# Recommendation tower: ScalarE makes part of the one-hot units, transforms wait half by half, cycles start at odd quads, six MLP steps move ahead of the tail

## The chip, the cores and the metric

One core of a Trainium2 chip. The metric is the device time of one execution in microseconds, the median of three.

## The reference

2048 samples have 40 ids each, one into each of 40 tables of 32-wide rows. For every pair of fields the kernel computes a bilinear form with a matrix of its own, puts 16 dense values behind the 780 results, and runs a small MLP. Cut to what matters:

```python
e = jnp.stack([tbl_f[ids[:, f]] for f in range(40)], axis=1)     # (2048, 40, 32)
vi, vj = e[:, _I_IDX, :], e[:, _J_IDX, :]                        # 780 pairs
z = jnp.einsum('bke,kef,bkf->bk', vi, W, vj)                     # W: (780, 32, 32)
h = jnp.concatenate([z, dense_ctx], axis=1)                      # (2048, 796)
h = jnp.maximum(h @ W_top1 + b_top1, 0.0)                        # 512
h = jnp.maximum(h @ W_top2 + b_top2, 0.0)                        # 256
y = h @ W_top3
```

## The kernel before, in words

The samples go in four chunks of 512, which lie along the free axis. The fields go in ten groups of four, so that a group's embeddings are a tile eT of 128 x 512.

A **quad** is up to four blocks of pairs. TensorE **transforms** (L567): four fp32 matmuls on 32 rows each, two into one PSUM bank pair (half 0) and two into the next (half 1); there are three such pairs. VectorE multiplies each half by the eT of the partner group into prods (L543), two **products** of 1024 columns a quad. TensorE **reduces** (L589): four matmuls with a 0/1 matrix add the products into zps. Eight quads fill a sum, which ScalarE drains into zs (L387). A chunk has 53 quads, numbered 0 to 52; 212 in all.

Tables with 1000 rows are **hot**: a hot group isn't gathered but looked up. For each of 8 **units** VectorE compares the group's shortened ids (L409, by ScalarE) with a code and writes a one-hot tile (L493), four slots in turn; TensorE multiplies it by the table in three bf16 parts, 12 matmuls (**look-up**, L616); after unit 7 ScalarE drains the bank mlp_ps into eT (L423). The chunks have 4, 3, 2 and 2 hot groups. The other 29 (chunk, group) pairs are gathered by GpSimd, 16 indirect DMAs each, and transposed by VectorE (L500).

The **MLP** of a chunk runs while the next chunk's quads go on, in **steps** (one k of one output tile, L636), two or three in a batch, through the one bank mlp_ps, which the look-ups share. The last chunk's MLP is the **tail**, in seven banks, after the last quad.

The order is written out by hand. TensorE and ScalarE go by **cycles** of two quads, at an even number over all 212. A table SIDES gives each quad its look-ups and MLP steps, MAKES the units to be made behind its products, 2 quads ahead of the look-up for units made in chunk 0 and 4 in the others; both engines with waits work strictly in their order. Without MLP steps a cycle is transform, reduction of the quad before, look-up, transform, reduction, look-up; with steps it is transform, steps, transform, two reductions. Where a cycle starts with the first quad of a sum, its last step goes between the reductions, as zps must be drained first. A transform waits once, for the first half of the quad before it to be multiplied (`wait(pe, multiplied, 2 * at - 1)`). The hot table of group 3 lies in the room of the MLP's first weights (w1s), which ScalarE loads after the last look-up that reads it.

## Time and profile before

| | us |
|---|---|
| median of 3 runs | 696.76 (696.74 to 699.01) |
| the profiled execution | 699.06 |
| its span, first to last instruction | 697.2 |
| TensorE busy in the span | 644.0 |
| VectorE busy | 580.5 |
| ScalarE busy | 70.1 |
| GpSimd busy (gathers) | 460.5 |

Busy is the time in which an engine had an instruction in work. What follows from the rows is worked out against the span, and carried over to the median as a difference.

### The profile page before, as it was taken

The numbers are of one execution on the slowest core, as the hardware profiler recorded it, in microseconds if no ns is written. First come the engines' busy times: TensorE is split into PE (matmuls) and PEld (weight loads), VectorE is DVE, ScalarE is ACT, GpSimd is POOL, SyncE is SP. The second block draws the span as 40 slices with busy tenths as digits, with TensorE's granted clock in tenths as the row PEclk, the third lists the DMA queues.
The fourth block names the chain that finished last, engine by engine and source line by source line (L and its number), as shares of the span: only waits on it lengthen the run. The fifth ranks groups of instructions, "written<-read, shape, count | busy, mean of one in ns | idle before, by whom it ended". The sixth has DMA issues, their size and how long they took to land.

```text
span 697.2 us, 11003 instructions
## 1 busy us (share of the span) xinstructions
PE 644.0 (92%) x4800; PEld 187.3 (27%) x4800; DVE 580.5 (83%) x578; ACT 70.1 (10%) x87; POOL 460.5 (66%) x471
## 2 busy tenths in 40 slices
PE   3898988988999999999999999998999999999898
PEld 1232222222223322322222222222222222222143
DVE  6988999999978799889877889889888888888800
ACT  5502001000100100110000000100000000000002
POOL 6777777777777777777777777777777777500000
PEclk9999999999999999999999999999999999999999
DMA  8735202000000110200000200000101000000000
GB/s 322 276 98 194 69 13 74 14 13 14 13 14 15 32 58 13 74 14 13 15 13 15 76 14 14 13 14 14 16 14 15 14 14 13 12 1 1 1 0 1
DMA packets 18944, 28.28 MB, mean 41 GB/s; under 512 B 8448, under 2 KB 16016, under 8 KB 17232
## 3 DMA queue, kind: packets, MB, share of 16 engines
q0 software_dynamic: 14848, 7.63, 7.4%
q1 hardware_dynamic: 3296, 17.57, 6.5%
q10 hardware_dynamic: 752, 2.37, 0.9%
q8 instruction: 38, 0.62, 0.4%
q14 instruction: 10, 0.08, 0.0%
HBM read 27.53 MB, written 0.01 MB: 40 GB/s over the span
## 4 chain that ended last, share of the span: by engine, by line
PE 61%; DVE 34%; issue 3%; DMA 1%; ACT 1%; ACTq 0%; SPq 0%; DVEq 0%
DVE prods L543 26%; PE tps L567 25%; PE zps L589 15%; PE mlp_ps L636 15%; DVE hot L493 6%; PE tps L636 4%; PE mlp_ps L616 2%; DMA ids<-in_hot_ids 1%; DVE eT L500 1%; PE zps L576 1%; DVE parts L482 0%; DVE zs L482 0%; ACTq L467 0%; ACT ids L409 0%; DVE w1s L482 0%
## 5 line engine op out<-in xcount | busy, mean ns | idle before, releaser
L543 DVE TENSOR_TENSOR prods<-tps,eT 128x1024 f32<-128x1024 f32 (+1 forms) x440 | 495.1, 1168 | 72.5 <-PE tps L567 68.8
L371 POOL DMA_INDIRECT rows<-in_table,idx x464 | 459.9, 991 | 144.4 <-issue 141.2
L567 PE MATMUL tps<-eT,weights 32*128 32x512 f32 x1680 | 242.4, 641 | 33.4 <-DVE prods L543 31.1
L589 PE MATMUL zps<-prods,select 128*32 128x512 f32 x1680 | 217.7, 605 | 2.3 <-DVE prods L543 1.5
L567 PEld LDWEIGHTS tps<-eT,weights 32*128 32x128 f32 x1680 | 66.7, 183 | 185.3 <-DVE prods L543 146.4
L636 PE MATMUL mlp_ps<-zs,w1s 128*128 128x512 f32 x182 | 89.8, 615 | 0.0
L589 PEld LDWEIGHTS zps<-prods,select 128*32 128x32 f32 x1680 | 38.2, 108 | 159.4 <-DVE prods L543 98.7
L616 PE MATMUL mlp_ps<-hot,parts 128*32 128x512 bf16 x960 | 65.2, 389 | 14.7 <-DVE hot L493 10.9
L493 DVE TENSOR_SCALAR hot<-ids,code 128x2048 bf16<-128x2048 int16 (+1 forms) x88 | 67.4, 787 | 1.9 <-ACT ids L409 1.6
L387 ACT ACTIVATE zs<-zps 128x512 f32<-128x512 f32 x28 | 16.7, 598 | 326.3 <-PE zps L589 326.3
L636 PEld LDWEIGHTS mlp_ps<-zs,w1s 128*128 128x128 f32 x182 | 31.3, 189 | 55.1 <-issue 55.1
L616 PEld LDWEIGHTS mlp_ps<-hot,parts 128*32 128x32 bf16 x960 | 27.1, 99 | 66.4 <-issue 37.0
L636 PE MATMUL mlp_ps<-h1s,w2s 128*128 128x512 f32 x48 | 24.1, 620 | 0.0
L394 ACT ACTIVATE h1s<-mlp_ps,b1s 128x512 f32<-128x512 f32 x13 | 8.9, 688 | 145.0 <-PE mlp_ps L636 145.0
L500 DVE STREAM_TRANSPOSE eT<-rows 128x512 f32<-128x512 f32 x29 | 20.3, 701 | 0.0
L409 ACT ACTIVATE ids<-ids 128x2048 int16<-128x2048 int32 x10 | 19.0, 1903 | 2.5 <-issue 2.5
L636 PE MATMUL tps<-zs,w1s 128*128 128x512 f32 x42 | 19.2, 592 | 0.0
L423 ACT ACTIVATE eT<-mlp_ps 128x512 f32<-128x512 f32 x11 | 6.6, 597 | 70.5 <-PE mlp_ps L616 70.4
L636 PEld LDWEIGHTS mlp_ps<-h1s,w2s 128*128 128x128 f32 x48 | 8.0, 189 | 15.2 <-issue 13.7
L636 PEld LDWEIGHTS tps<-zs,w1s 128*128 128x128 f32 x42 | 8.0, 190 | 10.0 <-issue 10.0
L394 ACT ACTIVATE h2s<-mlp_ps,b2s 128x512 f32<-128x512 f32 x6 | 4.1, 688 | 60.7 <-PE mlp_ps L636 60.7
L616 PE MATMUL mlp_ps<-hot,w1s 128*32 128x512 bf16 x96 | 7.6, 440 | 0.0
(31 smaller groups left out, 50.4 us busy)
## 6 DMA issues: line engine op xcount, KB each, us to landing
ids<-in_hot_ids SPq DMA_DIRECT2D x10, 1024.0 KB
rows<-in_table,idx POOLq DMA_INDIRECT x464, 2.4
zs<-in_hot_table SPq DMA_DIRECT2D x4, 512.0 KB, 7.5
w1s<-in_w ACTq DMA_DIRECT2D x1, 1792.0 KB, 7.6
weights<-in_wt SPq DMA_DIRECT2D x1, 1088.0 KB
...
```

The lines of the kernel that those rows point to most:

```text
L371: pool.indirect_dma_start(rows[:, k % ROW_SLOTS, m * EMB:(m + 1) * EMB], None, table, bass.IndirectOffsetOnAxis(ap=idx[:, g, t, m:m + 1], ...
L387: act.activation(zs[:, t % 2, kt, :], zps[:, :], ACT.Copy).then_inc(z_drained, 1)
L394: act.activation(dst[:, m, :], banks[out_tile], ACT.Relu, bias=bias[:, m:m + 1]).then_inc(mlp_drained, 1)
L409: act.activation(ids16[:, h % 2].rearrange("p q c -> p (q c)"), wide_ids[h], ACT.Copy).then_inc(ids_short, 1)
L493: dve.tensor_scalar(hot[:, (h * UNITS + u) % HOT_SLOTS], ids16[:, h % 2] if short else ids32[:, :, :], code[:, u:u + 1], None, ALU.is_equa ...
L500: dve.transpose(eT[:, (t * GROUPS + g) % ET_SLOTS, :], rows[:, k % ROW_SLOTS, :]).then_inc(transposed, 1)
L543: last = dve.tensor_tensor(prods[:, at % PROD_SLOTS, r:to + 1, :], tps[:, pair, r % 2:to % 2 + 1, :], eT[:, (t * GROUPS + c) % ET_SLOTS, : ...
L567: last = pe.matmul(tps[:, (2 * at + half) % PAIR_BANKS, r % 2, :], weights[part, n, :], eT[part, slot, :], start=True, stop=True)
L576: pe.matmul(zps[EMB * r:EMB * (r + 1), :], place[:, r, :], dense_s[:, :], start=True, stop=False)
L589: last = pe.matmul(zps[EMB * r:EMB * (r + 1), :], select[:, off:off + EMB], prods[:, at % PROD_SLOTS, r, :], start=kt < KT - 1 and n == fi ...
L616: last = pe.matmul(mlp_ps[EMB * q:EMB * (q + 1), :], part_of[g][part][:, col:col + EMB], hot[:, at % HOT_SLOTS, q, :], start=u == 0 and pa ...
L636: last = pe.matmul(banks[out_tile], [w1s, w2s][layer][:, k, m * PART:(m + 1) * PART], [zs[:, t % 2, k, :], h1s[:, k % M1, :]][layer], star ...
```

## The change

Seven things, in the order of the diff. Chunk 1 has 4 hot groups, its group 3 first, so that w1s is free after that one; 28 pairs are gathered, and eT has 14 slots instead of 13. The cycles are, in each chunk, quad 0 alone and then the pairs (1, 2), (3, 4) and so on; the case with a step between the reductions is gone, and a cycle with a single step has its reduction ahead of it. The batches of the MLP stand in one cycle after another, in chunk 3 too, where they were spread. Six steps of the last chunk's MLP (tile 0, k from 0 to 5) stand at quads 37, 39, 41, 43, 45 and 51 of chunk 3 instead of in the tail. ScalarE makes units 0, 2, 3, 5 and 6 of chunk 1's groups and the odd ones of chunks 2 and 3, in two activations: |id - code|, and relu(1 - that), which is 1 for equal integers and 0 otherwise. All units are made 4 quads ahead. And each half of a transform waits for itself: half 0 for the products one and a half quads back, half 1 as the whole did before.

```diff
@@ -81,7 +81,7 @@
-ROW_SLOTS, ET_SLOTS, PROD_SLOTS = 6, 13, 3
+ROW_SLOTS, ET_SLOTS, PROD_SLOTS = 6, 14, 3
 PAIR_BANKS = 3
@@ -104,8 +104,9 @@
 HOT_GROUPS = len(HOT_FIELDS) // Q
-HOT_COUNT = (4, 3, 2, 2)
-HOTS = [(t, g) for t in range(CHUNKS) for g in range(HOT_COUNT[t])]
+HOT_COUNT = (4, 4, 2, 2)
+HOTS = [(t, g) for t in range(CHUNKS) for g in ((3, 0, 1, 2) if t == 1 else range(HOT_COUNT[t]))]
 GATHERED = [(t, g) for t in range(CHUNKS) for g in range(HOT_COUNT[t], GROUPS)]
@@ -126,7 +127,12 @@
     return cut
+CYCLES = [at for t in range(CHUNKS) for at in [(t * QUADS,)] + [(t * QUADS + n, t * QUADS + n + 1) for n in range(1, QUADS, 2)]]
 def plan_sides():
@@ -141,26 +147,42 @@
         hots = [h for h, (t_, _) in enumerate(HOTS) if t_ == t + 1]
-        cycles = [at for at in range(0, TOTAL, 2) if t * QUADS <= at < (t + 1) * QUADS]
+        twos = [cycle[0] for cycle in CYCLES if len(cycle) == 2 and cycle[0] // QUADS == t]
         first = 3 * M1
...
         blocks += steps[first:] + [(h, u) for h in hots[1:] for u in range(0, UNITS, 2)]
-        for k, block in enumerate(blocks):
-            at = cycles[k if hots else k * len(cycles) // len(blocks)]
+        for at, block in zip(twos, blocks):
             if isinstance(block, tuple):
...
                 sides[at] += block
+    for k, n in enumerate(EARLY_AT):
+        sides[(CHUNKS - 1) * QUADS + n].append(("mlp", CHUNKS - 1, 0, 0, k))
     return sides
+EARLY_AT = (37, 39, 41, 43, 45, 51)
 SIDES = plan_sides()
-MADE_AHEAD = (2, 4, 4, 4)
+EARLY = [("mlp", CHUNKS - 1, 0, 0, k) for k in range(len(EARLY_AT))]
+def by_scalar(h, u):
+    return HOTS[h][0] == 1 and u not in (1, 4, 7) or HOTS[h][0] > 1 and u % 2 == 1
+def made_until(h, u, scalar):
+    return sum(by_scalar(h_, u_) == scalar for h_ in range(len(HOTS)) for u_ in range(UNITS) if (h_, u_) <= (h, u))
+MADE_AHEAD = 4
 MAKES = {at: [] for at in range(TOTAL)}
@@ -168,14 +190,12 @@
         if item[0] == "hot" and item[1] >= HOT_COUNT[0]:
-            MAKES[side_at - MADE_AHEAD[side_at // QUADS]].append(item[1:])
+            MAKES[max(side_at - MADE_AHEAD, min(side_at, 4))].append(item[1:])
 def steps_of(at):
-    steps = [item for item in SIDES[at] if item[0] == "mlp"]
-    return steps, int(len(steps) > 0 and at % QUADS % PER_KT == 0)
+    return [item for item in SIDES[at] if item[0] == "mlp"]
...
@@ -405,7 +430,8 @@
                 act.wait_ge(hot_ids_loaded[h % 2], 16 * (h // 2 + 1))
-                wait(act, hot_made, (h - 1) * UNITS)
+                if h >= 2:
+                    act.wait_ge(hot_made_dve, made_until(h - 2, UNITS - 1, False))
                 act.activation(ids16[:, h % 2].rearrange("p q c -> p (q c)"), wide_ids[h],
@@ -415,6 +441,17 @@
                 act.activation(part_of[g][part], raw_parts[g], ACT.Copy).then_inc(rounded, 1)
+            def make_unit(h, u):
+                if u == [by_scalar(h, u_) for u_ in range(UNITS)].index(True):
+                    act.wait_ge(ids_short, h + 1)
+                act.wait_ge(hot_used, h * UNITS + u - HOT_SLOTS + 1)
+                columns = hot[:, (h * UNITS + u) % HOT_SLOTS].rearrange("p q c -> p (q c)")
+                act.activation(columns, ids16[:, h % 2].rearrange("p q c -> p (q c)"), ACT.Abs,
+                               bias=minus_code[:, u:u + 1]).then_inc(distances, 1)
+                act.wait_ge(distances, made_until(h, u, True))
+                act.activation(columns, columns, ACT.Relu, scale=-1.0, bias=ones[:, 0:1]).then_inc(hot_made_act, 1)
             def drain_hot(h):
@@ -445,26 +482,31 @@
             round_part(3, 1)
+            act.wait_ge(code_built, 1)
+            act.activation(minus_code[:, :], code[:, :], ACT.Copy, scale=-1.0).then_inc(codes_turned, 1)
+            act.wait_ge(codes_turned, 1)
+            act.wait_ge(consts_built, 2 + Q)
             shorten(3)
-            for at in range(0, TOTAL, 2):
+            for cycle in CYCLES:
+                at = cycle[0]
                 if at in SHORTENED_AT:
                     shorten(SHORTENED_AT[at])
-                if at == QUADS // 2 * 2:
+                if at == QUADS:
                     act.wait_ge(mlp_loaded, 16 * 5)
-                steps, between = steps_of(at)
-                if not between:
-                    drain_tiles(steps)
+                drain_tiles(steps_of(at))
                 drain_sums(at - 1)
-                if between:
-                    drain_tiles(steps)
-                drain_sums(at)
-                for kind, *step in SIDES[at] + SIDES[at + 1]:
+                if len(cycle) == 2:
+                    drain_sums(at)
+                for kind, *step in [item for quad in cycle for item in SIDES[quad]]:
                     if kind == "hot" and step[1] == UNITS - 1:
                         drain_hot(step[0])
-                        if step[0] == HOT_COUNT[0] - 1:
+                        if HOTS[step[0]] == (1, HOT_GROUPS - 1):
                             for dst, src in ((w1s, w1), (w2s, w2), (w3s, w3), (b1s, b1), (b2s, b2)):
                                 act.dma_start(dst[:], src).then_inc(mlp_loaded, 16)
+                for unit in [unit for quad in cycle for unit in MAKES[quad]]:
+                    if by_scalar(*unit):
+                        make_unit(*unit)
             drain_z(CHUNKS - 1, KT - 1)
@@ -487,11 +529,11 @@
                     dve.wait_ge(code_built, 1)
-                elif u == (2 if h == 0 else 0):
+                elif u == (2 if h == 0 else [by_scalar(h, u_) for u_ in range(UNITS)].index(False)):
                     dve.wait_ge(ids_short, h + 1)
...
                 dve.tensor_scalar(hot[:, (h * UNITS + u) % HOT_SLOTS], ids16[:, h % 2] if short else ids32[:, :, :],
-                                  code[:, u:u + 1], None, ALU.is_equal).then_inc(hot_made, 1)
+                                  code[:, u:u + 1], None, ALU.is_equal).then_inc(hot_made_dve, 1)
             def transpose(k):
...
@@ -558,8 +602,9 @@
                 groups_there(pe, t, n)
-                wait(pe, multiplied, 2 * at - 1)
                 for half in range(2):
+                    wait(pe, multiplied, 2 * at + half - PAIR_BANKS + 1)
                     for r in (2 * half, 2 * half + 1):
@@ -604,9 +649,13 @@
                     bank_free(("hot", h))
-                pe.wait_ge(hot_made, at + 1)
+                if by_scalar(h, u):
+                    pe.wait_ge(hot_made_act, made_until(h, u, True))
+                else:
+                    pe.wait_ge(hot_made_dve, made_until(h, u, False))
                 for part in range(PARTS_OF):
@@ -647,30 +696,33 @@
             pe.wait_ge(consts_built, 1 + Q)
-            for at in range(0, TOTAL, 2):
-                steps, between = steps_of(at)
-                if at == QUADS // 2 * 2:
+            for cycle in CYCLES:
+                at = cycle[0]
+                steps = steps_of(at)
+                if at == QUADS:
                     pe.wait_ge(mlp_loaded, 16 * 5)
+                together = len(steps) > 1
                 transform(at)
-                for _, t, layer, m, k in steps[:len(steps) - between]:
+                if not together and at > 0:
+                    reduce(at - 1)
+                for _, t, layer, m, k in steps:
                     mlp(t, between_banks, layer, m, k)
-                if not steps and at > 0:
+                look_ups(at)
+                if len(cycle) == 2:
+                    transform(at + 1)
+                if together:
                     reduce(at - 1)
-                look_ups(at)
-                transform(at + 1)
-                if steps:
-                    reduce(at - 1)
-                for _, t, layer, m, k in steps[len(steps) - between:]:
-                    mlp(t, between_banks, layer, m, k)
-                reduce(at)
-                look_ups(at + 1)
+                if len(cycle) == 2:
+                    reduce(at)
+                    look_ups(at + 1)
             reduce(TOTAL - 1)
...
                     for m in range(outs):
-                        mlp(CHUNKS - 1, last_banks, layer, m, k)
+                        if ("mlp", CHUNKS - 1, layer, m, k) not in EARLY:
+                            mlp(CHUNKS - 1, last_banks, layer, m, k)
```

ScalarE at the start of chunk 0, before. The ids (L409) are those of hot group 3 of chunk 0 and, five DMA issues later, of the first hot group of chunk 1:

```order
L409 ACTIVATE ids<-ids 128x2048 [waits hot_made,hot_ids_loaded1]
L423 ACTIVATE eT<-mlp_ps 128x512 [waits hot_used] x2
L467 DMA w1s<-in_w 128x3584
L467 DMA w2s<-in_w 128x1024
L467 DMA w3s<-in_w 128x2
L467 DMA b1s<-in_b 128x4
L467 DMA b2s<-in_b 128x2
L409 ACTIVATE ids<-ids 128x2048 [waits hot_made,hot_ids_loaded0]
L387 ACTIVATE zs<-zps 128x512 [waits reduced,remainder]
```

The same place in the changed kernel, up to the first drained sum (L412); L451 and L454 are the two activations of a unit:

```order
L435 ACTIVATE ids<-ids 128x2048 [waits hot_ids_loaded1,hot_made_dve,consts_built,codes_turned]
L460 ACTIVATE eT<-mlp_ps 128x512 [waits hot_used]
L435 ACTIVATE ids<-ids 128x2048 [waits hot_made_dve,hot_ids_loaded0]
L460 ACTIVATE eT<-mlp_ps 128x512 [waits hot_used]
L451 ACTIVATE hot<-ids,minus_code 128x2048 [waits hot_used,ids_short]
L454 ACTIVATE hot<-hot,ones 128x2048 [waits distances]
L451 ACTIVATE hot<-ids,minus_code 128x2048 [waits hot_used]
L454 ACTIVATE hot<-hot,ones 128x2048 [waits distances]
L451 ACTIVATE hot<-ids,minus_code 128x2048 [waits hot_used]
L454 ACTIVATE hot<-hot,ones 128x2048 [waits distances]
L412 ACTIVATE zs<-zps 128x512 [waits reduced,remainder]
```

The second conversion stands ahead of the second drain now, the DMA issues are further down (behind the drain of the first hot group of chunk 1), and three units stand ahead of the first sum.

TensorE at the start of chunk 2, before. L567 is the transform, L636 an MLP step, L589 the reduction:

```order
L567 MATMUL tps<-eT,weights 128x512 x4
L636 MATMUL mlp_ps<-zs,w1s 128x512
L567 MATMUL tps<-eT,weights 128x512 x4
L589 MATMUL zps<-prods,select 32x512 x4
L636 MATMUL mlp_ps<-zs,w1s 128x512
L589 MATMUL zps<-prods,select 32x512 x4
L567 MATMUL tps<-eT,weights 128x512 x2
L636 MATMUL mlp_ps<-zs,w1s 128x512 x2
L567 MATMUL tps<-eT,weights 128x512 x4
L589 MATMUL zps<-prods,select 32x512 x6
L567 MATMUL tps<-eT,weights 128x512 x4
```

And in the changed kernel, from chunk 2's second quad on:

```order
L612 MATMUL tps<-eT,weights 128x512 x4
L685 MATMUL mlp_ps<-zs,w1s 128x512 x2
L612 MATMUL tps<-eT,weights 128x512 x2
L634 MATMUL zps<-prods,select 32x512 x8
L612 MATMUL tps<-eT,weights 128x512 x4
L685 MATMUL mlp_ps<-zs,w1s 128x512 x2
L612 MATMUL tps<-eT,weights 128x512 x4
```

The step between two reductions is gone; each cycle is transform, steps, transform, reductions of two quads.

TensorE around quad 43 of chunk 3, before:

```order
L567 MATMUL tps<-eT,weights 128x512 x4
L589 MATMUL zps<-prods,select 32x512 x4
L567 MATMUL tps<-eT,weights 128x512 x4
L589 MATMUL zps<-prods,select 32x512 x4
L567 MATMUL tps<-eT,weights 128x512 x4
L636 MATMUL mlp_ps<-h1s,w2s 128x512 x2
L567 MATMUL tps<-eT,weights 128x512 x4
L589 MATMUL zps<-prods,select 32x512 x8
```

And in the changed kernel, around the first two of the six steps that came out of the tail, quads 36 to 39:

```order
L612 MATMUL tps<-eT,weights 128x512 x4
L634 MATMUL zps<-prods,select 32x512 x4
L685 MATMUL mlp_ps<-zs,w1s 128x512
L612 MATMUL tps<-eT,weights 128x512 x4
L634 MATMUL zps<-prods,select 32x512 x4
L612 MATMUL tps<-eT,weights 128x512 x4
L634 MATMUL zps<-prods,select 32x512 x4
L685 MATMUL mlp_ps<-zs,w1s 128x512
L612 MATMUL tps<-eT,weights 128x512 x4
```

A batch of two steps of the MLP of chunk 2 stood here in every second or third cycle; now a single step of the last chunk's does.

TensorE with its waits, a quad of chunk 0 with a look-up, before:

```order
L567 MATMUL tps<-eT,weights 128x512 [waits multiplied]
L567 MATMUL tps<-eT,weights 128x512 x3
L589 MATMUL zps<-prods,select 32x512 [waits multiplied]
L589 MATMUL zps<-prods,select 32x512 x3
L616 MATMUL mlp_ps<-hot,parts 32x512 [waits hot_made,hot_drained]
L616 MATMUL mlp_ps<-hot,parts 32x512 x11
```

And in the changed kernel:

```order
L612 MATMUL tps<-eT,weights 128x512 [waits multiplied]
L612 MATMUL tps<-eT,weights 128x512
L612 MATMUL tps<-eT,weights 128x512 [waits multiplied]
L612 MATMUL tps<-eT,weights 128x512
L634 MATMUL zps<-prods,select 32x512 [waits multiplied]
L634 MATMUL zps<-prods,select 32x512 x3
```

The transform's four matmuls have a second wait in their midst, on the same semaphore.

## Rows read from the trace of the kernel before

**Rows 1.** The page, busy time of each engine, share of the span and instructions.
```profile
PE 644.0 (92%) x4800; PEld 187.3 (27%) x4800; DVE 580.5 (83%) x578; ACT 70.1 (10%) x87; POOL 460.5 (66%) x471
```

**Rows 2.** Windows: chunk 0 from quad 5, chunk 3, the tail (clock, DMA, GB/s last).
```profile
55.20:189.20 134.00, 119.84 (x1060) 31.90 (x1064) 130.25 (x131) 8.98 (x11) 102.89 (x103) 0.99 0.17 43
...
510.20:661.50 151.30, 143.44 (x928) 39.03 (x920) 128.55 (x118) 8.59 (x14) 72.34 (x77) 1.00 0.06 9
661.50:697.20 35.70, 32.89 (x96) 13.96 (x96) 0.00 (x0) 5.00 (x8) 0.00 (x0) 1.00 0.00 1
```

**Rows 3.** Groups by line and form, ScalarE (busy us, mean ns | idle before).
```profile
L409 ACT ACTIVATE ids<-ids 128x2048 int16<-128x2048 int32 x10 | 19.0, 1903 | 2.5 <-issue 2.5
L387 ACT ACTIVATE zs<-zps 128x512 f32<-128x512 f32 x28 | 16.7, 598 | 326.3 <-PE zps L589 326.3
L394 ACT ACTIVATE h1s<-mlp_ps,b1s 128x512 f32<-128x512 f32 x13 | 8.9, 688 | 145.0 <-PE mlp_ps L636 145.0
...
L417 ACT ACT_TABLE_LOAD x1 | 1.3, 1283 | 0.8 <-PEq L731 0.8
```

**Rows 4.** Timeline of TensorE, chunk 0, quads 42 and 43 (start, us).
```profile
163.46 1.14 PE L567 MATMUL tps<-eT,weights 32*128 32x512 f32 x8 [0.47 <-DVE prods L543]
164.59 1.06 PE L589 MATMUL zps<-prods,select 128*32 128x512 f32 x8
165.47 0.83 PE L616 MATMUL mlp_ps<-hot,parts 128*32 128x512 bf16 x12
166.23 1.14 PE L567 MATMUL tps<-eT,weights 32*128 32x512 f32 x8
```

**Rows 5.** Timeline of VectorE, the same stretch.
```profile
162.19 4.80 DVE L543 TENSOR_TENSOR prods<-tps,eT 128x1024 f32<-128x1024 f32 x4
166.91 0.74 DVE L493 TENSOR_SCALAR hot<-ids,code 128x2048 bf16<-128x2048 int16 x1
167.57 4.80 DVE L543 TENSOR_TENSOR prods<-tps,eT 128x1024 f32<-128x1024 f32 x4
```

**Rows 6.** Timeline of TensorE, chunk 1, a cycle with two MLP steps.
```profile
295.04 1.98 PE L636 MATMUL mlp_ps<-h1s,w2s 128*128 128x512 f32 x4
296.95 1.14 PE L567 MATMUL tps<-eT,weights 32*128 32x512 f32 x8
298.02 1.92 PE L589 MATMUL zps<-prods,select 128*32 128x512 f32 x16
299.88 1.14 PE L567 MATMUL tps<-eT,weights 32*128 32x512 f32 x8
```

**Rows 7.** Timeline of VectorE, chunk 1, quads with look-up and unit.
```profile
319.50 2.34 DVE L543 TENSOR_TENSOR prods<-tps,eT 128x1024 f32<-128x1024 f32 x2
...
325.35 2.35 DVE L543 TENSOR_TENSOR prods<-tps,eT 128x1024 f32<-128x1024 f32 x2
```

**Rows 8.** Timelines of ScalarE and VectorE at 52 us; window of 38 to 40.
```profile
52.46 1.91 ACT L409 ACTIVATE ids<-ids 128x2048 int16<-128x2048 int32 x1 [2.47 <-issue]
...
54.41 0.87 DVE L493 TENSOR_SCALAR hot<-ids,code 128x2048 bf16<-128x2048 int16 x1 [1.61 <-ACT ids L409]
...
38.00:40.00 2.00, 1.78 (x12) 0.46 (x12) 2.00 (x4) 0.00 (x0) 1.54 (x2) 0.94 0.15 27
```

**Rows 9.** Timelines, chunk 2: VectorE around 375 us, TensorE at 351.
```profile
373.20 4.81 DVE L543 TENSOR_TENSOR prods<-tps,eT 128x1024 f32<-128x1024 f32 x4 [0.64 <-PE tps L567]
379.77 2.36 DVE L543 TENSOR_TENSOR prods<-tps,eT 128x1024 f32<-128x1024 f32 x2 [1.76 <-PE tps L567]
...
351.34 1.13 PE L636 MATMUL mlp_ps<-zs,w1s 128*128 128x512 f32 x2
352.39 1.07 PE L589 MATMUL zps<-prods,select 128*32 128x512 f32 x8
```

**Rows 10.** Timeline of TensorE, the tail.
```profile
679.81 1.02 PE L636 MATMUL mlp_ps<-zs,w1s 128*128 128x512 f32 x2
...
683.24 1.02 PE L636 MATMUL mlp_ps<-zs,w1s 128*128 128x512 f32 x2
```

19 lines of the change are left out of this document (13 added, 6 removed).

## The prediction

> **What bounds the kernel now.** I read the page's busy line first [rows 1]: TensorE has a matmul in flight for 92% of the span, VectorE works for 83%, ScalarE for 10%. So neither of the first two can be made faster alone for long, and ScalarE is free. An average hides who waits where, so next come the stretches [rows 2]: chunk 0 from its quad 5 on takes 134.0 us, in which VectorE works 130.3; chunk 3 takes 151.3 with TensorE at 143.4; after the last product TensorE works alone for 35.7 us. To price one step I read the timeline and take the time from the start of one block to the start of the next, with nothing between: reduction to look-up 0.88, look-up to transform 0.76 [rows 4]; transform to the next block 1.07 (296.95 to 298.02), two MLP steps 1.91, two reductions 1.86 [rows 6]; one MLP step alone 1.05 and a further one 0.86 [rows 9, 10].
>
> Two loops come out of it. Where VectorE has its 0.66 us unit in a quad, the quad takes 2.93, the next one 2.45, since the group of four products begins at 162.19, the unit at 166.91, the next group at 167.57 [rows 5]. But 166.91 - 162.19 is 4.72 for two quads, so the second needs only 4.72 - 2.45 = 2.27 of VectorE. The other 0.18 is a stall, and [rows 4] show it: TensorE waits 0.47 for a product, so it was free at 162.99, and starts the transform at 163.46, and the next product can't start before 164.6. In cycles with two MLP steps TensorE never stops: 1.07 + 1.91 + 1.07 + 1.86 = 5.91 for two quads [rows 6], against 2 x 2.27 = 4.54 on VectorE.
>
> **The change, part by part.** (a) *First units of chunk 1.* VectorE waits 1.61 us at 54.41 for the shortened ids, and ScalarE started those at 52.46 only because it had stood 2.47 us behind five DMA issues [rows 8]. The ids themselves had come by about 38: from there the DMA engines are at 0.15 [rows 8]. The change shortens them ahead of the drain of group 3 and moves the five issues to the end of group (1, 3), some 12 quads on. That takes out 1.6 at least, one unit (0.66) goes to ScalarE, and the transform behind it isn't late. I take 3.0, with 1.6 and 4 as bounds.
>
> (b) *Chunk 0.* Units per look-up rise: 32 look-ups instead of 24 in 46 quads, 12 of their units on VectorE. A plain quad can now take VectorE's own 2.27, as the first half of a transform waits for products one and a half quads back. A quad with a look-up is set by the round product, reduction, look-up, transform, product: 0.14 + 0.88 + 0.76 + 1.07 + 0.07 = 2.92 after a plain one (0.14 and 0.07 are my estimates of the gaps before and after TensorE's part, from 163.46, where it starts some 0.05 after the product that began at 162.19 and takes 1.22, and from its end at 164.60), and TensorE's 1.07 + 0.88 + 0.76 = 2.72 after another look-up. VectorE's unit vanishes in the gap that this leaves. The pattern is two look-ups and a plain quad: 14 x 2.27 + 14 x 2.92 + 18 x 2.72 = 121.6. Before: 24 x 2.93 + 22 x 2.45 = 124.2. So 2.6 less, of which 2.0 to 2.5 go again: the dense rows' four matmuls (about one reduction, 0.9) lose their cover, and at quad 40 the drain of group (1, 1) stands behind the drain of quads 32 to 39 on ScalarE while the next look-up wants that bank: two drains of 0.60 [rows 3] and their gaps, 1.5. Net -0.5. Eight more look-ups therefore cost nothing to speak of; had they come on top it would be 8 x 0.76 = 6.1, the upper bound here.
>
> (c) *ScalarE's price.* No row shows Abs or a scaled Relu on 2048 columns. The nearest is the ids' Copy of 2048 columns, 1.90; a bias operand adds 0.688 - 0.598 = 0.09 [rows 3]. So 2 x 1.99 and two semaphore gaps, 4.1 a unit; the bounds are 3.9 and, if the second pass drags, 4.7. Chunk 0 holds 20 such units, 82 us, beside three conversions (5.7), four group drains (2.4), seven sum drains (4.2) and the five DMA issues (3): 97 of about 122 us. It fits, and a unit is made four quads, some 10.6 us, ahead.
>
> ScalarE shows one table load, of 1.28 us [rows 3], and the order of the changed program has no second one. The Trainium skill (ScalarE: Activation LUTs, What ACT_TABLE_LOAD costs) charges some 2.66 us for every switch to another table set, which would be over 5 us more a unit, 20 of them in chunk 0; but the same page (Table sets: the hidden batching unit) has relu, copy and abs in every set. By the first alone the sum would turn into a loss; by the second and the order nothing changes.
>
> (d) *Chunks 1 and 2, units.* Half of 16 units each leave VectorE. In the four quads with both a unit and a look-up, VectorE's two quads take 5.85 (319.50 to 325.35) [rows 7] and TensorE's 2 x 2.72 = 5.44: 0.41 a pair, two pairs a group, four groups, 3.3. In the pairs ahead (unit with MLP steps) both are near 5.9, and a transpose there (0.63) is in the way once or so a group; with one unit less TensorE's 5.91 covers it: 4 x 0.65 = 2.6. Together with small change -6.4; -3.3 if only the first half holds.
>
> (e) *Cycles that start at odd quads.* In chunk 2 a cycle with MLP steps that starts at the first quad of a sum splits its steps around the reductions: 373.20 to 379.77 is 6.57 [rows 9] against 5.91. The diff starts all cycles at n odd, so that this pattern is gone: three cycles at 0.66 and one with three steps at about 0.3, -2.3. Six plain quads at the chunks' ends fall from 2.45 to 2.27: -1.0.
>
> (f) *Chunk 3.* Its 17 batches now stand in 17 cycles in a row, then six cycles with one early step, three with none. By the rows: first quad 2.3; 12 x 5.91 + 4 x 6.77 (three steps) + 5.3 (the last batch, of short matmuls) = 103.3; a cycle with one step 2.27 + (0.14 + 1.0 + 1.05 + 1.07 + 0.07 = 3.33) = 5.60, six of them 33.6; three plain ones with the dense rows 3 x 4.54 + 1.0 = 14.6. Sum 153.8, against 151.3 [rows 2]: +2.5. So an early step costs about what it saves, and what pays for part of it is the split wait.
>
> (g) *Tail.* Each of the seven groups of four steps takes 683.24 - 679.81 = 3.43, 0.86 a step [rows 10]; six go: -5.1.
>
> (h) *Rest.* 28 gathered groups instead of 29, and a 14th slot: gathers wait for no slot before (GpSimd's idle time is its own issue gaps) and end long ahead of chunk 3's end, as GpSimd works 72.3 us in its 151.3 [rows 2]. Nothing. The cost of the added wait inside a transform: a second reduction follows a first in 0.86 to 1.0 with its own wait between [rows 6], so a wait that is met costs nothing; I take 0, the upper bound being 0.05 on each of 212 transforms, of which about 7 would show.
>
> Sum: -3.0 - 0.5 - 6.4 - 2.3 - 1.0 + 2.5 - 5.1 = -15.8. The profiled execution took 699.06 with a span of 697.2, the median is 696.76; the difference is carried over whole: 696.76 - 15.8 = 681.0, and I say 681.5.
>
> **Rivals.** *A, the halves don't come apart for free* (chance 0.10): the four matmuls of a transform run side by side, 8 records in 1.14 us [rows 4]. If the wait in their midst lets the second pair start late even when it is met, TensorE-bound cycles grow. For it: no row has a wait inside a transform. Against: the reductions of [rows 6]. At 0.05 each, +7 and the loss of (b) and (e)'s plain quads, +2: 691.
>
> *B, VectorE's relief is worth nothing* (0.08), as TensorE is busy anyway: only (a), (e)'s cycles, (f) and (g) remain, -3.0 - 2.3 + 2.5 - 5.1 and half of (f)'s plain quads: about -7, 690. For it the 92% of [rows 1]; against it the 5.85 against 5.44.
>
> *C, ScalarE is late* (0.05), which ends on the other side: chunk 0 leaves (122 - 15.3) / 20 = 5.3 us a unit. Up to there a late unit costs a few us; beyond it each us more a unit costs 20. At 6.1 us a unit the gain is gone, at 6.5 the time is 681.5 + 24 = 706. It needs activations at over 3 us where the nearest takes 1.90. The switch of tables of (c) is in this chance.
>
> *D, the change does all this and the clock falls* (0.02): [rows 8] show the granted clock at 0.94 from 38 to 40 after TensorE had idled at the start; more such stretches late would add some us; nothing points to them.
>
> **How the numbers follow.** My forecast has 0.75, with a range of its own of 677 to 686: (a) from -1.6 to -4, (b) up to 2 off each way, (d) down to -3.3, a unit at 4.7 us +2. Rivals A and B reach to 691 and are taken in, so that 676 to 690 leaves out C, part of A, and a little below. About 0.5%, 3.5 us, is what a measurement of this kernel tells from no change. Below 693.3 lie the forecast, B, most of A: 0.89; within 0.5% 0.06 (A with a larger price, C near its limit), slower 0.05 (C).
>
> **What would show it.** ScalarE's two new groups at about 2.0 us each, 36 of either, and ScalarE busy about 215 us. VectorE's product groups of four without a unit 4.6 long, not 4.8, in plain stretches. The wait of 1.61 at 54 us gone, and quad 6 about 3 us earlier. In chunk 0 VectorE waits for transforms in look-up quads, 0.4 to 0.7 each. In chunk 2 no cycle of 6.6. Last product to last instruction 30.6 instead of 35.7, and chunk 3 longer by 2 to 3. It would be wrong if TensorE's transform groups in MLP cycles grow beyond 1.07, or if look-ups wait for ScalarE in more places than one.

## The result and the profile after

The changed kernel takes 680.3 us (680.12 to 680.44, four runs), the kernel before beside it 697.8 (four runs, two at 696.7 and two at 698.9 and 699.0): ratio 0.974, 95% interval 0.9725 to 0.9759. The profiled execution took 680.44 with a span of 678.6, that of before 699.06 with 697.2.

The page of the changed kernel: the span, the busy line, and the groups that answer to [rows 1] and [rows 3]. In it L586 is the products, L612 the transforms, L634 the reductions, L665 the look-ups, L451 and L454 the two passes of a ScalarE unit, L412 the drain of a sum and L460 that of a looked-up group. In the variants below these numbers shift by a few lines, and the tile names stay.

```profile
span 678.6 us, 11237 instructions
PE 657.7 (97%) x4896; PEld 200.5 (30%) x4896; DVE 559.3 (82%) x550; ACT 213.9 (32%) x162; POOL 438.8 (65%) x455
L586 DVE TENSOR_TENSOR prods<-tps,eT 128x1024 f32<-128x1024 f32 (+1 forms) x440 | 492.9, 1169 | 81.5 <-PE tps L612 80.7
L451 ACT ACTIVATE hot<-ids,minus_code 128x2048 bf16<-128x2048 int16 x36 | 71.8, 1994 | 13.9 <-PE mlp_ps L665 12.2
L454 ACT ACTIVATE hot<-hot,ones 128x2048 bf16<-128x2048 bf16 x36 | 72.1, 2003 | 1.2
```

TensorE went from 92% to 97%. Read this with one caution: the wait now stands in the midst of a transform, and a transform that waits there is shown as one long group and counts as busy.

To see where the 18.6 us of span came from I cut both traces at the start of VectorE's first product of quad 0, quad 8, and of each chunk, and asked for windows. Before, quads 0 to 7, 8 to 52, chunks 1 and 2 (window, its length, then busy time of PE, PEld, DVE, ACT, POOL, the granted clock, DMA share, GB/s); chunk 3 and the tail are [rows 2]:

```profile
30.90:64.98 34.08, 29.89 (x312) 9.50 (x304) 29.41 (x34) 5.97 (x5) 26.46 (x26) 0.90 0.52 182
64.98:189.17 124.19, 111.29 (x996) 29.64 (x992) 121.26 (x121) 8.98 (x11) 95.22 (x96) 1.00 0.14 31
189.17:347.99 158.82, 154.90 (x1129) 45.16 (x1122) 138.00 (x133) 13.38 (x18) 121.31 (x124) 1.00 0.13 27
347.99:510.24 162.25, 156.23 (x1132) 44.38 (x1135) 139.25 (x135) 13.27 (x18) 123.52 (x128) 1.00 0.11 21
```

The same windows of the changed kernel, with chunk 3 and the tail:

```profile
31.45:60.39 28.94, 28.71 (x312) 9.69 (x304) 28.30 (x33) 17.62 (x12) 22.54 (x22) 1.00 0.42 145
60.39:183.13 122.74, 121.34 (x1088) 36.54 (x1080) 113.72 (x110) 77.83 (x48) 93.17 (x98) 1.00 0.21 59
183.13:338.29 155.16, 155.15 (x1130) 46.12 (x1128) 132.06 (x125) 44.96 (x34) 117.96 (x123) 1.00 0.13 28
338.29:493.45 155.16, 155.15 (x1130) 46.13 (x1128) 133.24 (x128) 44.96 (x34) 117.96 (x123) 1.00 0.11 21
493.45:648.02 154.57, 152.92 (x942) 43.84 (x940) 127.72 (x118) 8.58 (x14) 64.94 (x69) 1.00 0.06 8
648.02:678.60 30.58, 27.74 (x84) 11.69 (x84) 0.00 (x1) 5.00 (x8) 0.00 (x0) 0.98 0.00 0
```

The second number of each row is the length of the stretch. From before to changed it moves by -5.1 in quads 0 to 7 (which start 0.55 later), -1.4 in the rest of chunk 0, -3.7 in chunk 1, -7.1 in chunk 2, +3.3 in chunk 3 and -5.1 in the tail. The first row of before also has a granted clock of 0.90, where the changed kernel has 1.00.

### The profile page after: what moved, and what is told of

Read it like the earlier page. It is cut to its first block, busy times and chain, and to the rows that moved or that the text cites. A ratio compares the mean times of both kernels' runs of the same rounds, so it can differ in the third digit from the quotient of the medians.

```text
span 678.6 us, 11237 instructions
## 1 busy us (share of the span) xinstructions
PE 657.7 (97%) x4896; PEld 200.5 (30%) x4896; DVE 559.3 (82%) x550; ACT 213.9 (32%) x162; POOL 438.8 (65%) x455
## 4 chain that ended last, share of the span: by engine, by line
PE 94%; DVE 3%; DMA 1%; issue 1%; ACT 0%; SPq 0%; DVEq 0%
PE tps L612 35%; PE zps L634 30%; PE mlp_ps L685 16%; PE mlp_ps L665 8%; PE tps L685 4%; DVE hot L535 1%; DMA ids<-in_hot_ids 1%; DVE prods L586 1%; PE zps L621 1%; DVE zs L524 0%; PE mlp_ps L690 0%; DVE parts L524 0%; DVE w1s L524 0%; ACT eT L460 0%; ACT h2s L419 0%
## 5 line engine op out<-in xcount | busy, mean ns | idle before, releaser
L586 DVE TENSOR_TENSOR prods<-tps,eT 128x1024 f32<-128x1024 f32 (+1 forms) x440 | 492.9, 1169 | 81.5 <-PE tps L612 80.7
L396 POOL DMA_INDIRECT rows<-in_table,idx x448 | 438.1, 978 | 139.5 <-issue 136.3
L612 PE MATMUL tps<-eT,weights 32*128 32x512 f32 x1680 | 258.4, 640 | 1.0 <-ACT eT L460 0.8
L634 PE MATMUL zps<-prods,select 128*32 128x512 f32 x1680 | 215.2, 602 | 1.9 <-DVE prods L586 1.5
L612 PEld LDWEIGHTS tps<-eT,weights 32*128 32x128 f32 x1680 | 77.0, 182 | 149.9 <-DVE prods L586 84.1
L634 PEld LDWEIGHTS zps<-prods,select 128*32 128x32 f32 x1680 | 38.6, 108 | 157.8 <-DVE prods L586 91.7
L665 PE MATMUL mlp_ps<-hot,parts 128*32 128x512 bf16 x960 | 66.3, 395 | 15.2 <-DVE hot L535 11.1
L412 ACT ACTIVATE zs<-zps 128x512 f32<-128x512 f32 x28 | 16.7, 597 | 193.6 <-PE zps L634 193.6
L451 ACT ACTIVATE hot<-ids,minus_code 128x2048 bf16<-128x2048 int16 x36 | 71.8, 1994 | 13.9 <-PE mlp_ps L665 12.2
L454 ACT ACTIVATE hot<-hot,ones 128x2048 bf16<-128x2048 bf16 x36 | 72.1, 2003 | 1.2
L665 PEld LDWEIGHTS mlp_ps<-hot,parts 128*32 128x32 bf16 x960 | 27.6, 100 | 66.9 <-issue 33.9
L535 DVE TENSOR_SCALAR hot<-ids,code 128x2048 bf16<-128x2048 int16 (+1 forms) x60 | 44.6, 772 | 1.1 <-DMA ids<-in_hot_ids 0.9
L435 ACT ACTIVATE ids<-ids 128x2048 int16<-128x2048 int32 x11 | 20.9, 1902 | 2.4 <-DMA ids<-in_hot_ids 2.3
L460 ACT ACTIVATE eT<-mlp_ps 128x512 f32<-128x512 f32 x12 | 7.2, 597 | 38.3 <-PE mlp_ps L665 38.2
L665 PE MATMUL mlp_ps<-hot,w1s 128*32 128x512 bf16 x192 | 13.0, 379 | 0.0
```

Source lines behind the costliest of these rows:

```text
L396: pool.indirect_dma_start(rows[:, k % ROW_SLOTS, m * EMB:(m + 1) * EMB], None, table, bass.IndirectOffsetOnAxis(ap=idx[:, g, t, m:m + 1], ...
L412: act.activation(zs[:, t % 2, kt, :], zps[:, :], ACT.Copy).then_inc(z_drained, 1)
L435: act.activation(ids16[:, h % 2].rearrange("p q c -> p (q c)"), wide_ids[h], ACT.Copy).then_inc(ids_short, 1)
L451: act.activation(columns, ids16[:, h % 2].rearrange("p q c -> p (q c)"), ACT.Abs, bias=minus_code[:, u:u + 1]).then_inc(distances, 1)
L454: act.activation(columns, columns, ACT.Relu, scale=-1.0, bias=ones[:, 0:1]).then_inc(hot_made_act, 1)
L535: dve.tensor_scalar(hot[:, (h * UNITS + u) % HOT_SLOTS], ids16[:, h % 2] if short else ids32[:, :, :], code[:, u:u + 1], None, ALU.is_equa ...
```

## Experiments

**Five kernels on chips with pauses.** These were to be compared by their times.

e1, the split wait undone in the changed kernel:
```diff
-                    wait(pe, multiplied, 2 * at + half - PAIR_BANKS + 1)
+                    if half == 0:
+                        wait(pe, multiplied, 2 * at - 1)
```


> The changed kernel, but a transform again waits once, ahead of its first half, for the products of two quads back (the split wait alone is undone). My theory is that of a loop in which the 0.18 us lost in a plain quad is partly given back in the look-up quads behind it: about +2.3 us against the changed kernel, mostly in chunk 0 and in the single-step cycles of chunk 3. Rival, as the prediction had summed it: each plain quad counts for itself, 0.18 x 14 in chunk 0, 0.18 x 12 at the chunks' ends and 0.14 in each of six cycles with one early step, about +5.5. Rival A of the prediction (a wait in the midst of a transform costs 0.05 us even when it is met): -7 to -10 us, since 212 waits go, less what the stall costs again.

e2, the split wait alone, in the kernel before:
```diff
-                wait(pe, multiplied, 2 * at - 1)
                 for half in range(2):
+                    wait(pe, multiplied, 2 * at + half - 2)
```


> The kernel before with one part of the change: a transform waits for the products of each of its halves apart. Loop theory: about -5 us against before (the second quad of each pair in chunks 0 to 3 no longer stalls, of which a part is only moved into the next quad). Rival, each quad for itself: 22 x 0.18 in chunk 0 and some 25 plain or look-up quads in chunks 1 to 3, about -9. Rival B (VectorE's or TensorE's relief is worth nothing): 0 to -1. Rival A (the split costs something itself): positive, up to +7.

e3, `EARLY_AT = ()` in the changed kernel:


> The changed kernel with all 28 MLP steps of the last batch behind the last product, no early steps in chunk 3. The prediction said that an early step costs about what it saves. By its rows: tail +5.1, and in chunk 3 six single-step cycles of 5.60 become plain pairs of 4.54, -6.4: -1.3 us against the changed kernel. Rival, the early steps are hidden work and pay: +5.1 for the tail with chunk 3 unchanged, between +3 and +5.

e4, `together = len(steps) > 0` in the changed kernel:


> The changed kernel, with cycles of one early step ordered as those of two (transform, step, transform, then both reductions, where now the first reduction comes ahead of the step). Loop theory: VectorE's next product then waits for transform, step, transform alone and not for the reduction too; six cycles shrink from 5.6 to 5.1: about -3 us against the changed kernel. Rival, what an early step costs is TensorE time and not its place: 0, or +1 if the two reductions behind one another hold up the product buffers.

e6, `by_scalar` always False in the changed kernel:


> The changed kernel with all units made on VectorE (32 + 32 units, ScalarE makes none); orders, early ids, split wait, odd cycles, early steps as changed. Theory of the prediction: VectorE's second unit in a look-up pair shows. Chunk 0 has then 20 units more on VectorE (13.2 us of work, of which about 6 fall into gaps that TensorE leaves anyway), chunks 1 and 2 lose the 6.4 us of term (d) and a little of the plain quads: +11 to +12 us against the changed kernel, 692. Rival B of the prediction (VectorE's relief is worth nothing, as TensorE is busy anyway): 0 to +2.

Measured: on these chips the kernel before takes 1124 to 1126 us, and the ratios to it are e1 1.004 (1.0007 to 1.0077), e2 1.007 (1.0033 to 1.0104), e3 1.004 (1.0000 to 1.0072), e4 1.010 (1.0033 to 1.0161), e6 0.995 (0.9909 to 0.9991). No expectation can be read from that. The timeline of e1 shows why:

```profile
301.32 0.83 PE L666 MATMUL mlp_ps<-hot,parts 128*32 128x512 bf16 x12
302.08 1.14 PE L613 MATMUL tps<-eT,weights 32*128 32x512 f32 x8
...
308.55 2.00 ACT L451 ACTIVATE hot<-ids,minus_code 128x2048 bf16<-128x2048 int16 x1 [4.19 <-remote]
...
312.71 1.22 DVE L586 TENSOR_TENSOR prods<-tps,eT 128x1024 f32<-128x1024 f32 x1 [9.76 <-remote]
...
314.08 2.09 PE L613 MATMUL tps<-eT,weights 32*128 32x512 f32 x8 [9.86 <-issue]
```

TensorE, VectorE and ScalarE stand for 4 to 10 us, while GpSimd goes on with a gather every 1.25 us. The order of the waits shows where a pause starts. ScalarE's next unit needs the slot that the look-up of 301.32 frees, and VectorE's product needs the transform of 302.08. By the trace both were through by 303.2, but their semaphores are updated only at 308.46 and 312.68, and each engine starts at once then. TensorE's own next transform waits for that product and starts when it ends. So it is TensorE's signal that comes late; what holds it back is not shown. Over the whole span the clock is down to 0.82. Such pauses come at about the same quads in each of these runs (14, 21, 28, 35, 42 of chunk 0), and none of over 6 us begins after the last gather, which ends at 947 to 963 us. So the last 36 quads are undisturbed, and where the code is the same they repeat the first chip's to 0.01 us (103.17 us in e6 and in the changed kernel). Windows from quad 37 of chunk 3 to the last product, in the changed kernel, e1, e3 and e4, and the tail of e3:

```profile
603.86:648.02 44.16, 42.52 (x270) 11.18 (x268) 37.75 (x36) 1.20 (x2) 0.00 (x0) 1.00 0.00 1
```
```profile
1049.62:1093.98 44.36, 40.34 (x268) 9.16 (x268) 38.42 (x35) 1.19 (x2) 0.00 (x0) 1.00 0.00 1
```
```profile
1047.60:1086.02 38.42, 36.96 (x258) 9.76 (x256) 37.48 (x36) 1.19 (x2) 0.00 (x0) 1.00 0.00 1
1086.02:1121.80 35.78, 32.89 (x96) 13.97 (x96) 0.00 (x0) 5.00 (x8) 0.00 (x0) 1.00 0.00 0
```
```profile
1045.41:1087.08 41.67, 41.25 (x270) 11.98 (x268) 37.63 (x36) 1.19 (x2) 0.00 (x0) 1.00 0.00 1
```

e3: without early steps these quads are 5.74 shorter and the tail 5.2 longer, so the six early steps cost 0.6 more than they save (1.3 was expected). The rival (hidden work that pays) falls. e4: -2.5, where -3 was expected; so part of what an early step costs is its place in the order. A single-step cycle takes 3.36 + 2.27 = 5.63 in the changed kernel, 2.27 + 3.10 = 5.37 in e4. e1: +0.2 over 16 quads, and the single-step cycle is 3.18 + 2.45, again 5.63: what the second quad gains by the split wait, the first one gives back. For e2 the last 36 quads point the same way in the kernel before: 100.08 against 101.62, -1.5, where the shortened quads gain 1.95 and those behind them give back 0.5. The whole of e1's +2.3 and of e2's -5 was not read here; z2 below measures the former. e6 is disturbed too, but quads 40 and 42 of chunk 2 stand clear in it: with the unit back on VectorE they take 2.89 and 2.93, in the changed kernel 2.42 and 2.43, and quad 41 keeps its 2.92 or 2.93. That is some 0.5 for a pair with a unit and a look-up, where term (d) had 0.41.

**Are the gathers the cause of the pauses?** Two kernels with the same cut, after and before:
```diff
-            for k, (t, g) in enumerate(GATHERED):
+            for k, (t, g) in enumerate(GATHERED[:ROW_SLOTS]):
...
-                dve.wait_ge(rows_gathered[k % ROW_SLOTS], (k // ROW_SLOTS + 1) * (16 * GATHERS))
+                dve.wait_ge(rows_gathered[k % ROW_SLOTS], 16 * GATHERS)
```


> The changed kernel, but only the first six of its 28 groups are gathered (96 of 448 indirect DMAs); the 22 later transposes read whatever the six row slots hold, so from chunk 0 on part of the numbers are stale. On the chips of the runs so far the kernel before takes 1124 us instead of 697, and their traces show pauses in which TensorE, VectorE and ScalarE all stand, none of them after the last gather. Theory: the pauses come with the indirect DMAs, so with six groups they end at about 150 us: 680 to 710 us plus what the first 130 us lose, some 700 to 780. Rival: the pauses belong to the chip and not to the gathers (code that comes late), then about 1100 again. No theory of the change itself is tested by this kernel alone; with its partner it gives the difference of the two kernels without the pauses.

> The kernel before, with the same cut: only the first six of 29 groups gathered, the later ones stale. If gathers carry the pauses: its difference to the changed kernel with the same cut should be the 17.5 us measured on the first chip, less what the disturbed first 130 us hide: 10 to 20 us. Rival: the change gains only in the one state, and the difference is within 3 us here.

Measured: 785.2 us (781.8 to 790.1; 700 to 780 was expected) and 797.4 (796.4 to 798.6), a difference of 12.2, on a chip where the kernel before takes 1126.6. The clock shows where the pauses end, in n1:

```profile
PEclk9875555799999999999999999999999999999999
```

Quads 1 and 2 alone take 47.5 and 50.1 us there, and from the ninth slice on (156 us) nothing is disturbed. So on these chips the pauses come with the indirect DMAs. In the last of them TensorE doesn't quite stand still: from 99 to 136 us it lets through one matmul of a look-up every 2.80 us, and the last gather ends at 132.24:

```profile
127.17 0.59 PE L665 MATMUL mlp_ps<-hot,w1s 128*32 128x512 bf16 x1 [2.21 <-issue]
129.97 0.59 PE L665 MATMUL mlp_ps<-hot,w1s 128*32 128x512 bf16 x1 [2.21 <-issue]
```

And the change keeps its gain: chunks 1 and 2 of n1, then of n2:

```profile
284.70:439.70 155.00, 154.99 (x1129) 46.06 (x1128) 131.92 (x125) 44.97 (x34) 0.00 (x0) 1.00 0.04 15
439.70:594.70 155.00, 154.99 (x1130) 46.06 (x1128) 133.10 (x126) 44.97 (x34) 0.00 (x0) 1.00 0.03 8
```
```profile
287.80:446.10 158.30, 154.88 (x1129) 45.20 (x1122) 137.30 (x134) 13.37 (x18) 0.00 (x0) 1.00 0.04 15
446.10:607.60 161.50, 156.15 (x1132) 44.25 (x1135) 138.07 (x135) 13.26 (x18) 0.00 (x0) 1.00 0.02 8
```

**Four kernels without any gather.** Each has, besides its edit:
```diff
-                for m in range(GATHERS):
-                    pool.indirect_dma_start(
...
+                pool.memset(rows[:, k % ROW_SLOTS, :], 0.5).then_inc(rows_gathered[k % ROW_SLOTS], 16)
```

z1, three edits that the readings so far point to:
```diff
-EARLY_AT = (37, 39, 41, 43, 45, 51)
+EARLY_AT = (37, 37, 39, 39, 51, 51)
...
-                together = len(steps) > 1
+                together = len(steps) > 0
...
-                drain_sums(at - 1)
-                if len(cycle) == 2:
-                    drain_sums(at)
-                for kind, *step in [item for quad in cycle for item in SIDES[quad]]:
-                    if kind == "hot" and step[1] == UNITS - 1:
-                        drain_hot(step[0])
+                for quad in cycle:
+                    if quad > at:
+                        drain_sums(at)
+                    elif at > 0:
+                        drain_sums(at - 1)
+                    for kind, *step in SIDES[quad]:
+                        if kind == "hot" and step[1] == UNITS - 1:
+                            drain_hot(step[0])
```


> The changed kernel without any gather (six row slots are filled once with a constant and every transpose reads one of them: all gathered embeddings are left out), and with three edits. The six early steps stand in three cycles of two (quads 37, 39, 51 of chunk 3) instead of six of one; a cycle with any step does both reductions behind the second transform; ScalarE drains a looked-up group that ends in a cycle's first quad ahead of the sum that the same cycle ends. If the pauses come with the indirect DMAs alone, this run has none, and quads 9 to 38 of chunk 0 and all of chunks 1 and 2 last as in the changed kernel on the first chip (155.2 us each). Expected of the edits: quad 40 of chunk 0 falls from 4.17 to about 2.7 (-1.5); in chunk 3 three cycles of 5.91 and three of 4.58 stand for six of 5.63, -2.3; 680.3 - 3.8 = 676.5 us if nothing else differs. Rival: the stall at quad 40 is not ScalarE's order but TensorE's own, then 0 there and about 678.

Measured: 675.65 us (675.14 to 676.36), where 676.5 was expected. There are no pauses, and chunks 1 and 2 take 155.04 each, as on the first chip; so these kernels can be read against the first chip's traces quad by quad. Quad 40 takes 2.78 instead of 4.17. The timelines at that place, first the changed kernel:

```profile
147.61 0.60 ACT L412 ACTIVATE zs<-zps 128x512 f32<-128x512 f32 x1 [9.40 <-PE zps L634]
148.11 0.59 ACT L460 ACTIVATE eT<-mlp_ps 128x512 f32<-128x512 f32 x1
...
148.75 0.83 PE L665 MATMUL mlp_ps<-hot,parts 128*32 128x512 bf16 x12 [1.21 <-ACT eT L460]
```
and z1:
```profile
145.97 0.60 ACT L456 ACTIVATE eT<-mlp_ps 128x512 f32<-128x512 f32 x1 [7.29 <-PE mlp_ps L662]
...
147.81 0.83 PE L662 MATMUL mlp_ps<-hot,parts 128*32 128x512 bf16 x12
```

The group's drain no longer stands behind the sum's, and the look-up starts at once. Chunk 3 takes 151.78, 2.8 less.

z2, one wait, as e1:


> The changed kernel without any gather (rows filled with a constant, gathered embeddings left out), and a transform waits once again, ahead of its first half. Read quad by quad against the changed kernel. Loop theory: a plain quad takes 2.45 instead of 2.27, but the next look-up quad gives most of that back (TensorE's round is shorter by what it waited), so chunk 0 is longer by 0.9, chunks 1 and 2 by 0.4 each, chunk 3 by 0.5, together +2.3: 682 to 683 us. Rival, the prediction's sum, where each plain quad counts by itself: chunk 0 +2.5, all +5.5. Rival A (a wait met in the midst of a transform costs something): quads with MLP steps get shorter than 2.93 and 2.98.

Measured: 682.47 us (682.39 to 682.52), +2.2 with a first product 0.5 earlier. Its chunk 0, then chunk 1, against 151.68 (28.94 + 122.74) and 155.16:

```profile
30.93:183.56 152.63, 142.33 (x1400) 40.93 (x1392) 142.71 (x143) 95.44 (x59) 0.00 (x0) 1.00 0.17 62
...
183.56:339.23 155.67, 153.62 (x1132) 45.09 (x1128) 132.14 (x124) 44.95 (x34) 0.00 (x0) 1.00 0.04 15
```

By chunk it is +0.9, +0.5, +0.5 and +0.6, as the loop theory has it, and not 5.5. Against the chunks of n1, which is without gathers there as z2 is, it is +1.0, +0.6, +0.6 and +0.6, so the split wait is worth 2.5 to 2.8 us. A plain quad takes 2.45 for 2.27, and the look-up quad behind it 2.78 for 2.95. Quads with MLP steps keep their length, so a met wait in the midst of a transform costs nothing: rival A falls. TensorE's busy time is 142.3 in chunk 0, against 150.1 (28.71 + 121.34) in the changed kernel: that is the caution above in numbers.

z3, an edit for each of three chunks:
```diff
-CYCLES = [at for t in range(CHUNKS) for at in [(t * QUADS,)] + [(t * QUADS + n, t * QUADS + n + 1) for n in range(1, QUADS, 2)]]
+CYCLES = [at for t in range(CHUNKS) for at in [(t * QUADS,)] * (t != 2) + [(t * QUADS + n, t * QUADS + n + 1) for n in range(int(t != 2), QUADS - 1, 2)] + [(t * QUADS + QUADS - 1,)] * (t == 2)]
...
-    return HOTS[h][0] == 1 and u not in (1, 4, 7) or HOTS[h][0] > 1 and u % 2 == 1
+    return HOTS[h][0] == 2 or HOTS[h][0] == 3 and u % 2 == 1
```


> The changed kernel without any gather (gathered embeddings left out), and a different edit in each of three chunks, read by the lengths of the chunks (in the changed kernel 151.7, 155.1, 155.1). Chunk 0: VectorE makes all 32 units of chunk 1: theory of relief +6 (the second unit of a pair shows), rival B 0 to +1. Chunk 1: ScalarE makes all 16 units of chunk 2 instead of 8: a group of eight then takes 8 x 4.05 = 32 us where eight quads take 22, so look-ups wait for ScalarE, +8 a group, +16 in all; rival: the four quads of lead and ScalarE's idle time take it up, 0 to +4. Chunk 2: cycles start at even quads again, the last quad alone: +2.3 by the prediction's term (e), up to +5 as the split cycles also shift the look-up pairs; rival 0.

Measured, 708.6 us, chunks 0, 1 and 2:
```profile
30.70:187.89 157.19, 154.35 (x1396) 47.64 (x1384) 153.79 (x162) 17.55 (x19) 0.00 (x0) 1.00 0.16 59
187.89:359.95 172.06, 158.67 (x1131) 45.39 (x1129) 127.29 (x117) 75.46 (x50) 0.00 (x0) 0.98 0.04 13
359.95:520.04 160.09, 156.43 (x1130) 45.74 (x1128) 133.16 (x127) 44.93 (x34) 0.00 (x0) 1.00 0.02 8
```

Chunk 0 is 5.5 longer (+6 was expected): with all units VectorE works 153.8 of 157.2, so its relief was worth 5.5 us for 20 units, and rival B falls. Chunk 2 is 4.9 longer, twice term (e)'s 2.3. It doesn't isolate that term, as even cycles here lack the step between the reductions that the kernel before had, and as the look-up pairs shift too. Chunk 1 is 16.9 longer, close to the 16 that were expected, but by luck: ScalarE is busy for less than half of it. The two groups of look-ups, which run at ScalarE's 3.93 a unit, bring +3.4 and +4.6 and not 8 each, and 8.9 come from one quad (49, 12.6 instead of 3.7), which the timeline of ScalarE, TensorE and VectorE shows:

```profile
341.81 1.99 ACT L447 ACTIVATE hot<-ids,minus_code 128x2048 bf16<-128x2048 int16 x1
343.83 2.00 ACT L450 ACTIVATE hot<-hot,ones 128x2048 bf16<-128x2048 bf16 x1
345.74 0.58 ACT L408 ACTIVATE zs<-zps 128x512 f32<-128x512 f32 x1
...
346.37 1.93 PE L617 MATMUL zps<-dense_s,place 16*32 16x512 f32 x8 [6.44 <-ACT zs L408]
...
352.57 2.42 DVE L582 TENSOR_TENSOR prods<-tps,eT 128x1024 f32<-128x1024 f32 x3 [10.25 <-PE tps L608]
```

The sum drain of quads 40 to 47 stands behind the late units in ScalarE's queue, and TensorE's next reduction needs it. After the 6.44 us in which TensorE stood, the granted clock of the two windows from 342 to 354 is 0.72 and 0.71, and the blocks from the dense rows to the next transform take 5.0 us (346.37 to 351.37) that take 2.2 in the changed kernel. So some 2.8 of the 8.9 are the clock.

z4, the early ids alone, in the kernel before (`max(at // 2 * 2 - 4, 2)` for 4 in `SHORTENED_AT`):


> The kernel before without any gather (gathered embeddings left out), and ScalarE shortens the ids of chunk 1's first group at quad 2 instead of quad 4, ahead of the drain of group 3 and of its five DMA issues. Read quads 3 to 8 against the kernel before (starts 45.9, 50.4, 55.2, 58.3, 62.0, 65.0). Theory: only the 1.61 us wait at 54.4 goes, quad 4 from 4.76 to 3.1, and the stretch at half clock that follows TensorE's idling there (quad 6, 3.72) goes with it, -2.4 in all. Rival: the gain of the changed kernel at this place is the clock alone (quad 3, 4.57 against 2.99), and the early ids bring nothing where quad 3 still takes 4.57. About 694 us, with nothing else changed.

Measured: 694.1 us (692.4 to 694.3). Quad 4 takes 2.93 instead of 4.76 (-1.8) and quad 6 2.89 instead of 3.72 (-0.8), -2.6 in all, where the theory had -2.4. Quad 3 takes 3.04 instead of 4.57 (-1.5), so that the rival could not be read here; z1 settles it, where quad 3 takes 4.57 and quads 4 and 6 still take 2.93 and 2.96. The windows of 36 to 44 us tell quad 3 apart. Before:
```profile
36.00:40.00 4.00, 2.73 (x32) 0.74 (x24) 4.00 (x5) 0.60 (x1) 3.09 (x4) 0.97 0.50 185
40.00:44.00 4.00, 4.00 (x48) 1.76 (x44) 4.00 (x7) 0.00 (x0) 3.09 (x4) 0.60 0.08 12
```
z4:
```profile
36.00:40.00 4.00, 2.73 (x32) 0.74 (x24) 4.00 (x5) 1.67 (x2) 0.00 (x0) 1.00 0.41 168
40.00:44.00 4.00, 4.00 (x66) 1.67 (x60) 4.00 (x7) 0.84 (x1) 0.00 (x0) 1.00 0.54 190
```
z1, with the changed kernel's start:
```profile
40.00:44.00 4.00, 4.00 (x53) 1.65 (x42) 4.00 (x7) 0.00 (x0) 0.00 (x0) 0.65 0.72 256
```

TensorE had worked 2.73 of the 4 us ahead in before and in z4 alike, and the clock fell in one and not in the other; it fell in z1 (4.57 for quad 3), and not in the changed kernel (2.99). So the fall at quad 3 is not the change's, and it is worth some 1.6 us either way. Four runs of before at two levels, 696.7 and 699.0, with the profiled one at the upper, fit that. Such a fall isn't bound to that place: the profiled z4 has one at quad 41 of chunk 2, after TensorE had stood for 1.67 us, and its chunk 2 takes 163.15 where n2's takes 161.50. The window:
```profile
467.60:471.10 3.50, 3.50 (x16) 0.75 (x20) 3.04 (x4) 0.00 (x0) 0.00 (x0) 0.51 0.00 0
```

e9, the three edits of z1 in the whole kernel with all gathers:


> The whole changed kernel, with all gathers, and the three edits of the run without gathers (early steps in pairs, both reductions behind the second transform, a looked-up group drained ahead of the sum). On these chips the pauses hide a difference of 4 us, so the ratio to before should lie near 1.00 as that of the other variants; behind the last gather it should be exact: from quad 36 of chunk 3 to the end 71.9 us instead of 74.8 in the changed kernel. Rival: with the gathers the pairs lose what they gained, 74 to 75.

Measured: 1122.9 us (1117.1 to 1132.5) against 1125.5 (1106.7 to 1137.5), which the scatter doesn't tell apart, on a chip with pauses; behind the last gather it is as expected, 41.36 instead of 44.16 to the last product:

```profile
1047.58:1088.94 41.36, 40.74 (x270) 11.30 (x268) 37.82 (x36) 1.19 (x2) 0.00 (x0) 1.00 0.00 1
```

## Why the prediction was right

681.5 was said and 680.3 measured; against the lower level of before the change is -16.4, where the sum said -15.8. Term by term:

- (a) -3.0 for the start. The windows show -5.1 + 0.55 = -4.6, of which 1.6 is the clock at quad 3. z4 shows the early ids alone at -1.8 (quad 4) and -0.8 (quad 6, where the clock no longer falls); the last 0.4 was not tried apart. The mechanism held, and the size is the 3.0 that was said once the fall of the clock at quad 3 is taken off. That 0.8 of it is a gain in clock the prediction had not named.
- (b) -0.5, measured -1.4. The stall at quad 40 was forecast at 1.5, and z1 removes 1.4 of it. Without gathers the stretch takes 123.66 before (z4, n2) and 122.59 in the changed kernel (n1), -1.1; the other 0.4 goes with the gathers (below).
- (c) 4.1 us a unit; the passes take 1.994 and 2.003 and a unit in a queue 3.92 to 3.93, the lower bound. ScalarE is busy for 213.9, where 215 was said, and hardly ever late: eleven look-ups' weight loads wait for a unit of its, 0.3 us each, and no matmul does. That is more places than the one place that the prediction allowed before it would be wrong, but none leaves TensorE's matmuls idle. The trace has one table load for all its passes and drains, as before, so that nothing is paid for changing between them. Of the two rules of the Trainium skill (ScalarE: Activation LUTs) that the prediction weighed, the trace agrees with "Table sets: the hidden batching unit"; no run here shows the price of a switch.
- (d) and (e) in chunks 1 and 2, -6.4 - 2.3 - 1.0 = -9.7 (some of the 1.0 lies in the other chunks); measured -10.7 with gathers and (158.26 + 161.50) - (155.04 + 155.03) = -9.7 without. By chunk, without gathers, it is -3.2 and -6.5. So what chunk 2 gained beyond chunk 1 is 3.2, where (e)'s cycles had 2.3; how the rest splits between (d) and (e) was not tried apart, beyond the pairs in e6.
- (f) +2.5, measured +3.3. The single-step cycle was forecast at 5.60 and takes 5.63; where the other 0.8 stands I did not resolve. "An early step costs about what it saves" is right: e3 has it at 0.6 more.
- (g) -5.1, measured -5.1. (h) no cost for the added wait: z2. No cost of the 14th slot or the 28 groups shows in any window.

One step was priced too high. In (b), (e) and (f) each plain quad counts for itself, and by that the split wait would be worth 5.5 us. z2 has 2.5 to 2.8, since a loop of two engines gives back in one quad part of what it gained in the last. That the total came within 1.2 us all the same is in part luck: -1.1 in (b) for -0.5, 0.9 more in chunk 2 than (e) had, and the clock in (a) made up for it.

Of rival C the prediction had the limit (5.3 us a unit in chunk 0) but only part of the price. Where ScalarE gets late (z3, chunk 1), the look-ups that wait for units cost 8.0, and a drain that stands behind late units costs another 8.9, the clock that falls then included.

What stays open: the changed kernel itself was not run on a chip with pauses, so whether its gain survives there with all gathers isn't shown; its nearest variants (e1, e3, e4, e9) are no faster there than before. And z1's 4.7 us below the changed kernel (1.4 at quad 40, 2.8 in chunk 3, and 0.4 that go with the gathers) are shown without gathers, with all gathers only in the last 16 quads (2.8). What delays TensorE's signals in the pauses stays open too.
